# Low-rank product in six float16 products, and the second norm's rows turned by VectorE and a DRAM scratch

## The reference, cut to what matters

```python
# x: (2, 2048, 1024) float32, 4096 rows in all; 32 heads of 32
xn = layernorm(x)
q, k, v = xn @ wq.T + bq, xn @ wk.T + bk, xn @ wv.T + bv      # each as (B, S, H=32, D=32)
scores = einsum('bshd,bstd->bsht', q, k) / sqrt(32)            # between the heads of one row
x1 = x + einsum('bsht,bstd->bshd', softmax(scores), v)
x2 = layernorm(x1)
base = x2 @ base_w.T + base_b
gates = softmax over the best 2 of 8 of (x2 @ gate_w.T), scattered to w_full (B, S, 8)
low = einsum('bsd,erd->ebsr', x2, lora_A)                      # 8 experts of rank 16: 128 columns
out = x1 + base + 2.0 * einsum('ebsr,eor,bse->bso', low, lora_B, w_full)
```

## Time and profile before

| | us |
|---|---|
| median of 3 runs | 1314.05 (1313.95 to 1314.11) |
| the profiled execution | 1315.04 |
| its span, first to last instruction | 1313.2 |
| TensorE busy | 1286.7 (98%) |
| VectorE busy | 1106.1 (84%) |
| ScalarE busy | 672.4 (51%) |
| GpSimd busy | 278.7 (21%) |

### The profile page before, as it was taken

The page is one execution under the profiler, slowest core; times in us unless marked ns, Lnnn a source line. Parts: engine busy times, 40 slices in busy tenths (PEclk is TensorE's granted clock), DMA queues, the critical chain, the costliest instruction groups (busy, mean ns, idle before and its releaser), DMA issues.

```text
span 1313.2 us, 30329 instructions
## 1 busy us (share of the span) xinstructions
PE 1286.7 (98%) x12506; PEld 682.2 (52%) x12506; DVE 1106.1 (84%) x1576; ACT 672.4 (51%) x1029; POOL 278.7 (21%) x305
## 2 busy tenths in 40 slices
PE   6899999999999999999999999999999999999998
PEld 4554554555555455555555555555555555555554
DVE  5799888888988888888888888888888888888885
ACT  4865445555444555544555554455554445545431
POOL 0212211212221121222112122211222221222220
PEclk9899999999999999999999999999999999999999
DMA  9732332221233222233322223322212322221210
GB/s 361 265 82 65 82 80 64 64 64 60 67 80 80 62 66 58 55 78 80 80 58 70 55 57 80 80 71 65 72 50 62 80 80 64 68 74 49 48 50 33
DMA packets 162011, 103.72 MB, mean 79 GB/s; under 512 B 135616, under 2 KB 136640, under 8 KB 161984
## 3 DMA queue, kind: packets, MB, share of 16 engines
q1 hardware_dynamic: 161984, 103.36, 28.1%
HBM read 69.78 MB, written 16.78 MB: 66 GB/s over the span
## 4 chain that ended last, share of the span: by engine, by line
PE 88%; DVE 6%; DMA 2%; ACT 1%; issue 1%; SPq 0%; DVEq 0%; POOL 0%; ACTq 0%
PE acc L1291 24%; PE acc L1300 24%; PE dense_acc L1430 23%; PE attn_ps L1383 7%; PE dense_acc L1438 4%; PE attn_ps L1391 2%; DMA work<-wT_dram 2%; PE low_ps L1414 1%; PE low_ps L1413 1%; PE low_ps L1415 1%; PE dense_acc L1453 1%; DVE w_lo_k L864 1%; DVE base_parts L864 1%; DVE v_parts L864 0%; DVE work L967 0%
## 5 line engine op out<-in xcount | busy, mean ns | idle before, releaser
L1430 PE MATMUL dense_acc<-base_parts,x 128*128 128x512 f16 x1488 | 330.1, 379 | 0.0
L360 ACT COPY work<-work 32x512 f16<-32x512 f16 x380 | 233.5, 614 | 8.5
L1430 PEld LDWEIGHTS dense_acc<-base_parts,x 128*128 128x128 f16 x1488 | 143.2, 98 | 167.2 <-issue 0.5
L967 DVE SCALAR_TENSOR_TENSOR work<-acc,acc_to_a,biases_sb 128x512 f32<-128x512 f32 x192 | 143.6, 749 | 47.2 <-PE acc L1300 44.6
L1291 PE MATMUL acc<-w_hi_q,x_hi 128*128 128x512 f16 x496 | 118.7, 383 | 0.0
L532 POOL TENSOR_TENSOR work<-work 128x1024 f16<-128x1024 f32 x32 | 68.2, 2131 | 237.3 <-ACT work L754 233.3
L1291 PE MATMUL acc<-w_hi_k,x_hi 128*128 128x512 f16 x496 | 117.5, 380 | 0.0
L1300 PE MATMUL acc<-w_hi_q,x_lo 128*128 128x512 f16 x496 | 117.3, 379 | 0.0
L1300 PE MATMUL acc<-w_hi_k,x_lo 128*128 128x512 f16 x496 | 117.2, 379 | 0.0
L1291 PE MATMUL acc<-v_parts,x_hi 128*128 128x512 f16 x496 | 117.2, 379 | 0.0
L1300 PE MATMUL acc<-v_parts,x_lo 128*128 128x512 f16 x496 | 117.2, 379 | 0.0
(11 more groups left out here) (200 smaller groups left out, 2139.2 us busy)
## 6 DMA issues: line engine op xcount, KB each, us to landing
work<-x_dram SPq DMA_DIRECT2D x64, 512.0 KB, 3.5
work<-work SPq DMA_DIRECT2D x256, 64.0 KB, 2.0
work<-x_dram SPq DMA_DIRECT2D x124, 128.0 KB, 3.3
out_dram<-work SPq DMA_DIRECT2D x31, 512.0 KB, 2.9
work<-wT_dram SPq DMA_DIRECT2D x16, 512.0 KB, 9.5
v_parts<-wT_dram SPq DMA_DIRECT2D x8, 512.0 KB, 14.5
base_parts<-wT_dram SPq DMA_DIRECT2D x5, 512.0 KB, 10.3
biases_sb<-bias_dram SPq DMA_DIRECT2D x4, 512.0 KB, 10.9
```

The costliest lines, as they stand in the source:

```text
L360: copy(diag[c * QD:(c + 1) * QD, :, c, j::NQ, :], src).then_inc(vdiag_ready, 1)
L967: nc.vector.scalar_tensor_tensor(out=ev[:, s], in0=acc[bank][:, :], scalar=acc_to_a[:, i:i + 1], in1=bias[g][:, s], op0=ALU.mult, op1=ALU. ...
L1430: nc.tensor.matmul(dense_acc[n][:, :], rows_part[:, k, :], w_part[:, k, cols], start=(k == 0 and m == 0), stop=False)
```

## The change

1. **Low-rank product.** `lora_up` and `low` become a high and a low float16 part each (`lora_parts`, `low_parts`). For each half three products (high by high, high by low, low by high), six in all, where two float32 products stood. The low-rank matrix gets a scale of its own in step 0 (`gram_lora`, `base_scale`, `lora_high`, `lora_low`). In every tile ScalarE's `low_copy` writes the high part and a new VectorE instruction `low_low` the low part.
2. **Second norm's rows.** `turn2` leaves the loop (it stays in the tail). VectorE turns `xn` in blocks of 32 x 32 into `x2_flat` (the memory of `soft`), four transfers (`park_x2`: two from SP, two from ScalarE's queue, each 32 rows in 1024 pieces of 128 bytes) write it to a scratch in DRAM in the order that completes the turn, and one (`fetch_x2`, ScalarE's queue, 512 KB) reads it back. ScalarE casts it from there, and its low part goes from VectorE to GpSimd.
3. **Order.** The low part of q goes from GpSimd to VectorE (`second_low`), between the biases of the value halves. The context product is put into the first key half. `spread_stats` comes ahead of the query halves. `experts` is cut in two: the terms of x2's high part right behind the scores, those of the low part inside the base product. `gate_top` comes behind the shift of the scores. ScalarE's cast of the next x goes ahead of the cast of v, and `low_copy` behind the cast of the probabilities. VectorE waits for x2's low part ahead of the scores' top.
4. In step 0 and 1 the staging places of some weights and the order of their loads change.

The core of the diff:

```diff
+        x2_turned = sem("x2_turned")
+        x2_parked = sem("x2_parked")
+        x2_fetched = sem("x2_fetched")
+        turn_dram = nc.dram_tensor("turn_dram", (P, HID), F32, kind="Internal").ap()
+        parked = turn_dram.rearrange("(b c) (k q t) -> q c k b t", b=NQ, k=KC, q=NQ)
...
+        x2_flat = soft
+        x2_f32 = x2_flat.rearrange("p (k n) -> p k n", k=KC)
...
+        def park_x2(queue, p, quads):
+            queue.wait_ge(x2_turned, p + 1)
+            for q in quads:
+                src = x2_flat[q * QD:(q + 1) * QD, :].rearrange("c (k b t) -> c k b t", k=KC, b=NQ)
+                queue.dma_start(parked[q], src).then_inc(x2_parked, 16)
...
+                    park_x2(sp, t - 1, (0, 1))
...
+            def x2_low(p):
+                pool.wait_ge(x2hi_ready, p + 1)
+                nc.gpsimd.tensor_tensor(x2_lo, x2_f32, x2_hi, ALU.subtract).then_inc(x2lo_ready, 1)
...
+                x2_low(t - 1)
                 v_low(t)
...
-                    act.wait_ge(scored, t)
+                    act.wait_ge(v_acc, 2 * t)
...
             def x2_high(p):
-                act.wait_ge(turned2, p + 1)
-                nc.scalar.copy(x2_hi, rows_ps).then_inc(x2hi_ready, 1)
+                if isinstance(p, int) and p == T - 1:
+                    act.wait_ge(turned2, 1)
+                    nc.scalar.copy(x2_hi, rows_ps).then_inc(x2hi_ready, 1)
+                else:
+                    act.wait_ge(x2_fetched, 16 * (p + 1))
+                    nc.scalar.copy(x2_hi, x2_f32).then_inc(x2hi_ready, 1)
+            def fetch_x2(p):
+                act.wait_ge(x2_parked, 16 * NQ * (p + 1))
+                act.dma_start(x2_flat, turn_dram).then_inc(x2_fetched, 16)
...
-                nc.scalar.copy(low[:, :], low_ps[:, 2 * P:3 * P]).then_inc(lowt_ready, 1)
+                nc.scalar.copy(low_parts[:, 0, :], low_ps[:, 2 * P:3 * P]).then_inc(low_hi_ready, 1)
+            def lora_high():
...
+                park_x2(act, t - 1, (2, 3))
...
-                x2_high(t - 1)
+                fetch_x2(t - 1)
...
                 nc.scalar.copy(dense_parts[:, :, 0, :], turned3).then_inc(b_hi_ready, 1)
+                x2_high(t - 1)
+                if nxt:
+                    x1_high(t + 1)
...
-                for c in C_ACT_FIRST[:1]:
-                    spread_v(nc.scalar.copy, c)
-                if nxt:
-                    x1_high(t + 1)
-                    low_copy(t - 1)
-                for c in C_ACT_FIRST[1:]:
+                for c in C_ACT_FIRST:
...
+                    low_copy(t - 1)
                     for c in C_ACT_LAST:
                         spread_v(nc.scalar.copy, c)
...
+            def base_scale():
+                o = SCALED.index("base")
+                dve.wait_ge(norm_spread, o + 1)
+                nc.vector.tensor_reduce(w_max[:, BASE_:BASE_ + 1], norm_ps["base"], AX.X, ALU.add).then_inc(norm_ready, 1)
...
+            def lora_low():
+                dve.wait_ge(w_hi_act["ag"], 2)
+                nc.vector.scalar_tensor_tensor(out=lora_parts[:, 1, :], in0=lora_stage,
+                                               scalar=w_undo[:, LORA_:LORA_ + 1], in1=lora_parts[:, 0, :],
+                                               op0=ALU.mult, op1=ALU.subtract).then_inc(w_lo_done["ag"], 1)
+            def low_low(p):
+                dve.wait_ge(low_hi_ready, p + 1)
+                nc.vector.tensor_tensor(low_parts[:, 1, :], low_ps[:, 2 * P:3 * P], low_parts[:, 0, :],
+                                        ALU.subtract).then_inc(lowt_ready, 1)
...
+            def turn_x2(p):
+                dve.wait_ge(xn2_ready, p + 1)
+                dve.wait_ge(pt_ready, p + 1)
+                nc.vector.transpose(x2_flat, xn).then_inc(x2_turned, 1)
+            def second_low(t):
+                dve.wait_ge(b_hi_ready, t + 1)
+                nc.vector.tensor_tensor(dense_parts[:, :, 1, :], turned3, dense_parts[:, :, 0, :],
+                                        ALU.subtract).then_inc(b_lo_ready, 1)
...
+                    turn_x2(t - 1)
                     turn_first(t)
...
-                x2_low(t - 1)
...
+                second_low(t)
...
-                if prev:
-                    gate_top(t - 1)
                 dve.wait_ge(scored, t + 1)
+                dve.wait_ge(x2lo_ready, t)
                 scores = attn_ps[:, :].rearrange("p (t c) -> p t c", t=QD)
...
+                gate_top(t - 1)
                 if nxt:
                     gate_rest(t - 1)
...
                     x1_low(t + 1)
+                    low_low(t - 1)
                 for c in C_DVE if nxt else C_ACT_LAST + C_DVE:
...
+                    if k == 2 and inside is not None:
+                        inside()
...
+            def gram_lora():
+                pe.wait_ge(lora_loaded, 16)
+                pe.wait_ge(xlo_ready, 1)
+                part_of = top_halves(lora_stage)
+                for c in range(0, HID, P):
+                    part = part_of[:, c:c + P]
+                    mm = nc.tensor.matmul(gram_ps["lora"], part, part, start=(c == 0), stop=(c == HID - P))
+                mm.then_inc(gram_done, 1)
...
-            def experts(p):
+            def experts_high(p):
                 pe.wait_ge(x2hi_ready, p + 1)
-                pe.wait_ge(x2lo_ready, p + 1)
                 pe.wait_ge(lowt_ready, p + 1)
                 dst = low_ps[:, 0:AG]
                 for k in range(KC):
                     nc.tensor.matmul(dst, x2_hi[:, k, :], ag_hi[:, k, :], start=(k == 0), stop=False)
                     nc.tensor.matmul(dst, x2_hi[:, k, :], ag_lo[:, k, :], start=False, stop=False)
-                    mm = nc.tensor.matmul(dst, x2_lo[:, k, :], ag_hi[:, k, :], start=False, stop=(k == KC - 1))
+            def experts_low(p):
+                pe.wait_ge(x2lo_ready, p + 1)
+                for k in range(KC):
+                    mm = nc.tensor.matmul(low_ps[:, 0:AG], x2_lo[:, k, :], ag_hi[:, k, :], start=False,
+                                          stop=(k == KC - 1))
                 mm.then_inc(ag_acc, 1)
+            def experts(p):
+                experts_high(p)
+                experts_low(p)
...
             def dense_lora(p):
+                pe.wait_ge(low_hi_ready, p + 1)
+                pe.wait_ge(w_lo_done["ag"], 2)
+                halves = [slice(n * HALF, (n + 1) * HALF) for n in range(NB)]
+                for n, cols in enumerate(halves):
+                    for up_part in range(2):
+                        nc.tensor.matmul(dense_acc[n][:, :], low_parts[:, 0, :], lora_parts[:, up_part, cols],
+                                         start=False, stop=False)
                 pe.wait_ge(lowt_ready, p + 2)
-                pe.wait_ge(lora_loaded, 16)
-                for n in range(NB):
-                    nc.tensor.matmul(dense_acc[n][:, :], low[:, :], lora_up[:, n * HALF:(n + 1) * HALF],
+                for n, cols in enumerate(halves):
+                    nc.tensor.matmul(dense_acc[n][:, :], low_parts[:, 1, :], lora_parts[:, 0, cols],
                                      start=False, stop=True).then_inc(base_acc, 1)
+            def dense_half0(p):
+                pe.wait_ge(base_free, 2 * p + 1)
+                dense_terms(0, 0, 1, True)
+                experts_low(p)
+                dense_terms(0, 1, 3, False)
...
-                project(FIRST, 0, 0, a_acc)
                 one = isinstance(t, int) and t == 1
                 if one:
+                    project(FIRST, 0, 0, a_acc)
                     spread_flag(1)
                 else:
-                    context(t - 1)
+                    project(FIRST, 0, 0, a_acc, lambda: context(t - 1))
...
+                if nxt:
+                    spread_stats(t + 1)
+
                 pe.wait_ge(v_biased, 2 * t)
                 project(SECOND, 0, 2, b_acc)
-                if nxt:
-                    spread_stats(t + 1)
                 pe.wait_ge(a_biased, 2 * t + 1)
                 project(SECOND, 1, 0, b_acc)
-                turn2(t - 1)
                 pe.wait_ge(a_biased, 2 * t + 2)
                 project("v", 0, 1, v_acc)
                 pe.wait_ge(b_biased, 2 * t + 1)
                 project("v", 1, 2, v_acc)
-                experts(t - 1)
                 pe.wait_ge(ctx_turned, t)
                 pe.wait_ge(adiag_ready, 2 * 16 * NQ * (t + 1))
                 pe.wait_ge(b_lo_ready, t + 1)
                 attend(scored)
+                experts_high(t - 1)
                 if one:
+                    experts_low(0)
```

134 lines of the change are left out of this document (86 added, 48 removed).

## The result

The changed kernel takes **1345.5 us** (median of 4 runs, 1341.65 to 1348.06), the kernel before 1314.08 beside it: a ratio of 1.024 [1.022, 1.026], slower. I had forecast 1337 with a range of 1320 to 1385, and slower with 0.82. The profiled execution is the quickest of the four, 1341.65 us with a span of 1339.8; the granted clock is 0.994 in it and 0.989 to 0.991 in the other three, whose spans are 1343.0 to 1346.3.

What follows compares the result with a forecast made beforehand. TensorE bound the kernel before; after the change a tile-to-tile path through VectorE, ScalarE and TensorE would, at 39.1 us a tile. 1315.04 + 20 (loop) + 3 (ends) = 1338, against the median 1337 us; range 1320 to 1385.

Steps and rivals of the forecast that it cites:

- The ring (part 3): Tile-to-tile loop of key product, VectorE to shifted scores, ScalarE's exponential, spreads and low copy, low-rank products: 39.1 us; chance 0.50.
- TensorE's idle time: In a middle tile TensorE would idle some 1.2 us ahead of the low-rank products, and again ahead of the scores.
- The small waits: VectorE would wait 0.3 and 0.4 us for casts of k and q, over 2 for the key product; TensorE some 95%.
- The transfers (part 4): Scratch writes land 4.0 to 5.7 us after x2's turn, with 0.9 to 2.6 to spare: no cost.
- The ends (part 5): Outside the loop: +4 us for new VectorE work at the weights, -1 at the last tile, sum +3.
- rival 1: Issuing the scratch writes holds ScalarE: up to 0.9 us a tile more, 1345 to 1368 us; chance 0.20.
- rival 2: Small scratch writes are dear: at double price 42 us a tile, 1417 us; at half the excess 1375; chance 0.09.
- rival 3: VectorE's waits absorb its added work and TensorE stays the bound: 37.17 us a tile, 1279 us; chance 0.14.
- 4 (lock of GpSimd and VectorE): x2's low part on GpSimd and q's on VectorE lock each other out, up to 1.2 us: 1372 us; chance 0.03.

Runs made afterwards that it cites:

- e1: The changed kernel with the context product behind the first key half again, not inside it: 1321.06 us.
- e5: The changed kernel with two float32 low-rank products in place of the six float16 ones (low-rank output not the reference's): 1371.26 us.
- e3: The changed kernel with the context product behind the first key half and the low copy between ScalarE's first two spreads again, scratch kept: 1313.54 us.
- e7: The changed kernel with all four scratch writes issued by SP, none from ScalarE's queue: 1342.09 us.
- e8: The changed kernel with each of the four scratch writes issued twice, the extra one to a scratch nobody reads: 1486.72 us.
- e9: The kernel before with only the six float16 low-rank products on their own operands; no scratch, VectorE turn or new order: 1309.70 us.
- e12: As e9, but in step 1 VectorE makes the low half of the low-rank activations ahead of the next x's low part: 1309.41 us.
- e11: As e3, but VectorE turns the rows of the second norm behind the turn of the keys instead of ahead of it: 1369.66 us.

## Why the prediction was right, and where it was not

**The ring (part 3): right, term by term.** VectorE from the first bias addition to the end of the shift: 650.44 to 674.77, 24.3 us, 24.4 predicted. From there to the end of the low copy at 682.90: 8.1 against 8.2. Low-rank products, key product and context, to the next first bias addition at 689.47: 6.6 against 6.3 and 0.2 for handovers. The sum is 39.04 against 39.1. e1 shows it by taking a term out, e5 by making one longer.

**TensorE's idle time: the amount right, the place wrong.** 39.04 less 37.17 are 1.87 us. I had put 1.2 ahead of the low-rank products. There the rows show 0.3, and 1.53 ahead of the scores, ended by the diagonal copies. This changed nothing of the sum, since VectorE comes to the scores only at 672.33 when they are done at 670.79. But I read it as harmless, and it was the next bound: it is why e3 missed by 15 us.

**The small waits: right.** 0.40 and 0.33 for the casts of k and q (0.3 and 0.35), 2.40 for the key product (over 2), TensorE at 94% (some 95).

**The transfers (part 4): no cost in the change, as said.** The last write lands at most 5.1 us after the turn, within 4.0 to 5.7. That ScalarE's issues are hidden held by 0.2 us only. The low part of x2 on GpSimd ends at 671.39, 0.9 us ahead of need, the low end of the 0.9 to 2.6 that I gave. The read took 3.9, not 3.5. Against the Trainium skill (DMA: Bandwidth & Descriptors, Specifications), which speaks of a read and a modification below 512 bytes, stand two numbers: writes of 128 bytes land in 3.5 to 3.8 us (2.7 in e7) where reads of the same packets take 3.1 to 3.3, and the profile's count of HBM reads rises from 69.78 to 86.03 MB by the 16.25 of reading back alone, and not at all when the writes are doubled (86.03 again). No rewriting shows at the memory. What I had not priced at all is what these transfers do to others: 2.0 to 2.6 us for the diagonal copies.

**The ends (part 5): wrong.** I had +3; the rows show +6.4 and +3.4, near 10. At the front VectorE's own new work is near the 4 us that I counted: its busy time up to the key product of t = 2 is 111.4 against 105.5, and 1.7 of the difference is one instruction that was held. I did not see that the base bias, loaded later, puts GpSimd's addition beside VectorE's low part of x (2.86 instead of 1.18 in the kernel after), nor the low clock after the wait: after a wait of 2.38, the granted clock is 0.50 from 135 to 138, and the four low-rank products of step 1 take 1.89 where they take 1.04 in the loop. At the back I expected 1 us to be gained. Instead the maximum waits 1.44 for GpSimd's low part of x2 and the low half waits 0.72 for its copy ahead of the last turn.

**The size.** Loop +16.8 (20 predicted), ends +9.8 (3 predicted): 3.6 above my 1338 for the profiled execution. The other 4 us up to the median are the difference between the profiled execution and the rest. That the total came so near is in part luck: the loop came out 3 us below my figure (my own sum, 39.1 less 38.46, gives 18.6 and not 20) and the ends 7 above. The median even lies in the interval that I had given to rival 1, 1345 to 1368, though the period of 39.04 is that of the ring without it.

**Slips in the sums.** 1417 and 1375 of rival 2 leave out the 3 us of the ends that the other cases have (1420 and 1378), and rival 3 takes 2 for them. The range isn't touched.

**The rivals.** 1 (issuing holds ScalarE) did not occur, but with twice the writes it does: VectorE then waits 2.9 us a tile for the cast of the keys (e8). 2 (small writes are dear) is refuted by the landing times. 3 (work absorbed) is refuted by the period; e1 shows how near it was, though: moving the context product back gives three quarters of the loss back. 4 (lock of GpSimd and VectorE) did not occur where I had looked for it, and occurred in step 1. There I was also wrong on the trace of before: I wrote that such a pair does not overlap in it. In step 1 of that trace GpSimd's small addition at 96.37 takes 1.05 us instead of 0.19, beside VectorE's L1078 at 96.08.

## What to carry to other kernels

When one engine has 98% and the next 84%, walk the rings that close from tile to tile before shortening the first: here a ring that had 1.6 us of slack became the longest path, through VectorE's added work, the context inside the key product and the later low copy. Count for each inserted instruction what stands behind it, and for each transfer what it does to the landing of the others. Judge the parts alone: the six products by themselves give 0.5%. The loss came with the two moves of order, on top of VectorE's added work: with both taken back (e3) the kernel is level with before. VectorE's turn and the scratch, which take 0.87 us a tile off TensorE, gave the loop nothing: 38.05 in e3 with them, 38.04 in e9 without.

## What the runs showed of the hardware

- **GpSimd and VectorE, both with two inputs from SBUF, slow each other.** VectorE's low part of x takes 1.18 us alone, 2.86, 2.87 and 3.30 beside GpSimd's addition of 2.35, and in all three runs (after, e12, e9) it ends 1.07 to 1.08 us after that addition does, nearly its full time alone: it hardly advances until GpSimd is through. The record shows no idle time for it, only the longer duration. The other way round, in e3 in each middle tile, beside VectorE's residual addition:

```profile
640.96 1.29 DVE L1182 SCALAR_TENSOR_TENSOR work<-work,columns 128x1024 f32<-128x1024 f32 x1 [0.24 <-DVE work L1174]
```

```profile
641.25 1.05 POOL L547 TENSOR_TENSOR stat_rows<-row_stats,in_quad 128x8 f32<-128x8 f32 x1
```

  The same small addition takes 0.20 in the kernel after, where nothing of the kind runs beside it. It ends with VectorE's instruction (642.25 and 642.30). This agrees with the lock of the Trainium skill (SBUF — State Buffer, Who interferes with whom): the one that started first held the other, in both directions.
- **Transfers slow each other without a full queue.** The mean busy share of the DMA engines is 0.38 in the middle of the kernel after, and 0.26 in the earlier trace rows; still the 64 KB copies go from 2.0 to 2.6 us.
- **The third and fourth of four scattered issues in a row take 0.95 to 1.48 us** instead of 0.60, with both queues issuing at once (e8: 1.16 and 1.48 on ScalarE's, 0.95 and 1.24 on SP's). Four on SP's queue alone take 2.78 in all (e7).
- **TensorE's clock falls behind long waits and makes them dearer.** It was granted at 0.50 after idle stretches of 2.38 (after), 3.42 (e9) and 4.45 us (e8), and at 1.00 in the loop of the kernel after, with 1.53 us of waiting in every tile. What follows at the low clock takes up to twice as long, and so a wait off the critical ring can come onto it (e8, e11).
